# Two heads per stationary operand in the second score pass, its maxima subtracted by a bf16 matmul of three parts, and the experts' counts and lists put in other slots

## The reference: what is computed

```python
h = tok_ref(x, 102, tok_table, pos_table, seg_table)      # gather + position + segment, times 16
h = h + attn_ref(layernorm(h), wq, wk, wv, wgq, wgk, wgv, r_out_w, gate_local_w, gate_remote_w, w_out)
h = h + ffn_ref(layernorm(h), centroids, ln_g, ln_b, w1, b1, w2, b2)
```

## Time and profile before

| | |
|---|---|
| median of three runs | 2784.46 us (2783.8 to 2791.09) |
| the profiled execution | 2778.41 us, span 2776.6 us |
| PE busy | 2597.7 us, 94% of the span, 41512 matmul records |
| DVE busy | 1737.3 us, 63% |
| ACT busy | 1199.2 us, 43% |
| POOL busy | 966.5 us, 35% |
| attention, steady stretch | about 70 to 1690 us, 32 sequences |
| choice for expert 0 alone | about 1695 to 1775 us |
| experts | about 1785 to 2776 us |

### The profile page before, as it was taken

The page is one execution under the profiler, slowest core; times in us unless marked ns, Lnnn a source line. Parts: engine busy times, 40 slices in busy tenths (PEclk is TensorE's granted clock), DMA queues, the critical chain, the costliest instruction groups (busy, mean ns, idle before and its releaser), DMA issues. The chain is left out here.

```text
span 2776.6 us, 97280 instructions
## 1 busy us (share of the span) xinstructions
PE 2597.7 (94%) x41512; PEld 1766.3 (64%) x41512; DVE 1737.3 (63%) x5575; ACT 1199.2 (43%) x2659; POOL 966.5 (35%) x1417
## 2 busy tenths in 40 slices
PE   5999999999999999999999983399999999999998
PEld 3666666666766666666666662266666666666665
DVE  5666666666666666666666656775756667575600
ACT  2444445545444544444444430243333444433342
POOL 4332333433423333334233200134434343444333
PEclk9999999999999999999999995699999999999999
DMA  2110111101101111011010001012121121112020
GB/s 77 24 26 24 28 26 26 26 26 26 26 24 28 26 26 25 25 26 28 24 26 26 24 17 39 16 33 67 34 71 49 50 70 36 66 35 71 27 71 29
DMA packets 62599, 98.67 MB, mean 36 GB/s; under 512 B 13676, under 2 KB 47544, under 8 KB 62168
## 3 DMA queue, kind: packets, MB, share of 16 engines
q0 software_dynamic: 18624, 51.14, 6.9%
q1 hardware_dynamic: 43544, 41.29, 4.5%
HBM read 55.88 MB, written 33.82 MB: 32 GB/s over the span
## 5 line engine op out<-in xcount | busy, mean ns | idle before, releaser
L911 PE MATMUL banks<-hT,w 128*128 128x512 f32 x1024 | 469.8, 606 | 11.2 <-ACT hT L728 10.8
L1180 DVE TENSOR_REDUCE mx<-banks 128x8 f32<-128x1024 f32 x256 | 301.2, 1219 | 128.2 <-PE banks L1022 128.2
L702 ACT ACTIVATE probT<-banks 128x1024 f32<-128x1024 f32 x256 | 259.2, 1026 | 224.8 <-PE banks L1066 224.8
L739 ACT ACTIVATE hid<-banks,b 128x512 f32<-128x512 f32 x256 | 175.8, 687 | 400.9 <-PE banks L911 400.9
L911 PEld LDWEIGHTS banks<-hT,w 128*128 128x128 f32 x1024 | 188.0, 192 | 214.4 <-issue 198.5
L550 POOL TENSOR_TENSOR h<-ve,mhalf 128x2 f32<-128x2 f32 x128 | 92.0, 719 | 648.8 <-DVE ve L1221 648.7
L528 POOL DMA_INDIRECT rows<-in_tok_table,idx_now x132 | 138.4, 1049 | 399.9 <-DVE hres L1158 347.8
L1079 PEld LDWEIGHTS V_ps<-Ve,probT 128*64 128x64 f32 x4096 | 251.6, 139 | 34.6 <-issue 34.6
L1079 PE MATMUL V_ps<-Ve,probT 128*64 128x17 f32 x4096 | 264.4, 212 | 0.1
L1079 PE MATMUL V_ps<-Vo,probT 128*64 128x17 f32 x4096 | 264.4, 212 | 0.0
L593 POOL TENSOR_TENSOR orow<-orow,b 128x256 f32<-128x256 f32 x128 | 134.7, 1052 | 370.7 <-DVE orow L1345 369.6
(11 more groups left out here) (225 smaller groups left out, 5402.7 us busy)
## 6 DMA issues: line engine op xcount, KB each, us to landing
h_rows<-h SPq DMA_DIRECT2D x128, 130.0 KB, 2.0
w<-in_w SPq DMA_DIRECT2D x16, 1024.0 KB, 5.2
Qt<-low SPq DMA_DIRECT2D x512, 2.0 KB
Gq<-lowl SPq DMA_DIRECT2D x256, 2.0 KB
Kt<-units SPq DMA_DIRECT2D x256, 4.0 KB
rows<-in_tok_table,idx_now POOLq DMA_INDIRECT x132, 3.7
out_rows<-orow,idx_cur POOLq DMA_INDIRECT x128, 2.4
Gk<-units SPq DMA_DIRECT2D x64, 1.0 KB
```

The costliest lines, as they stand in the source:

```text
L702: nc.scalar.activation(dst[:, 2 * pair:2 * pair + 2, :], banks[:, 2 * pair:2 * pair + 2, :], ACT.Exp).then_inc(s_exp, 1)
L739: nc.scalar.activation(hid[:, m, :], S_ps[m % 2][:, 0:GT * P], ACT.Gelu_apprx_tanh, bias=b1[:, m:m + 1]).then_inc(s_hid, 1)
L911: mm = nc.tensor.matmul(S_ps[m % 2][:, 0:GT * P], w1[:, c, m * P:(m + 1) * P], hT[g % 2][:, c, :], start=c == 0, stop=c == KC - 1)
L1180: nc.vector.tensor_reduce(tops.rearrange("p (g h) -> p g h", g=2), banks[:, 2 * pair:2 * pair + 2, :].rearrange("p g (h k) -> p g h k", h= ...
```

## The change

Second pass of a query tile (steps 1 to 4). The even and odd head of a pair now share one stationary operand: `Kf`, the keys of all heads with nothing zeroed, is the stationary operand, and `Qt` (now with the other head's rows zeroed, by `c_query`) is streamed for both `j` at once. So 24 product matmuls stand where 48 stood, with twice the columns each. The first pass uses `Qf` (plain scaled queries) as its stationary operand and is otherwise as it was. ACT writes `Qf` and `Kf` besides the two copies of `Qt` and of `Kt` (three copies of 512 columns for each Q or K task instead of two).

The maxima no longer go through a DMA. DVE splits the negative maximum of each query and head into three bf16 parts (high, middle, rest; four instructions right behind the two reductions, in `dve_tops`), MX lays them out on PE (four bf16 matmuls against the identity `identb` instead of one transpose), ACT copies the whole bank to `tops_rows`, and `key_scores` adds them to the scores: for each strip one bf16 matmul of 3 rows, 128 output rows and 512 columns with ones as stationary operand, between the masks and the products. MX waits on the new semaphore `s_tops`. Step 0 keeps the old way under the name ML.

Experts: the radix sums on PE stand one or two slots later, the list has four pieces of 32 tiles (`LC = 4`), and its pieces stand in other slots.

```diff
-            [("MT", 1), ("ET", 0), ("ET", 1), ("WO", 1), ("VAL", 2), ("ET", 2), ("ET", 3), ("MX", 0)],
+            [("MT", 1), ("ET", 0), ("ET", 1), ("WO", 1), ("VAL", 2), ("ET", 2), ("ET", 3), ("ML", 0)],
...
             elif name == "MX":
-                dst = lowl if t == 0 else low[(t - 1) % 2]
-                nc.scalar.activation(dst[:, :], bank[0:LH * TS if t == 0 else H, 0:P], ACT.Copy, scale=-1.0).then_inc(s_mA, 1)
+                nc.scalar.activation(tops_rows[t % 2][:, :, :].rearrange("p n q -> p (n q)"), bank[:, :],
+                                     ACT.Copy).then_inc(s_mA, 1)
...
             elif name == "Q":
+                nc.scalar.activation(Qf[nx][:, t, :], bank[:, :], ACT.Copy, scale=HD ** -0.5)
                 for j in range(2):
-                    ins_ = nc.scalar.activation(Qt[nx][:, j, t, :], bank[:, :], ACT.Copy, scale=HD ** -0.5)
+                    ins_ = nc.scalar.activation(Qt[nx][:, j, t, :], bank[:, :], ACT.Copy, scale=c_query[:, j:j + 1])
...
             elif name == "K":
+                nc.scalar.activation(Kf[nx][:, t, W:], bank[:, :], ACT.Copy)
...
             elif name == "MX":
-                pe.wait_ge(s_max, 2 * (NU * b + t + 1))
-                tops = mxl[:, :] if t == 0 else mx[:, t % 2, :]
-                mm = nc.tensor.transpose(bank[0:LH * TS if t == 0 else H, 0:P], tops, c_ident)
+                pe.wait_ge(s_tops, TS * b + t)
+                for n in range(G):
+                    mm = nc.tensor.matmul(bank[:, n * P:(n + 1) * P], parts3[t % 2][:, n, :], identb[:, :], start=True, stop=True)
...
                 pe.wait_ge(s_max, drained)
-                pe.wait_ge(s_low[u], 16 * 2 * (1 + (TS if u == 0 else KC)) * (b + 1))
+                if u == 0:
+                    pe.wait_ge(s_low, 16 * (2 + 2 * TS) * (b + 1))
+                else:
+                    pe.wait_ge(s_mA, lowered)
...
-                for n in range(G):
-                    j, c = divmod(n, KC)
+                for g in range(G):
+                    nc.tensor.matmul(banks[:, g, :], onesb[32 * g:32 * g + 3, :],
+                                     tops_rows[(t + 1) % 2][32 * g:32 * g + 3, :, :].rearrange("p n q -> p (n q)"),
+                                     start=False, stop=False)
+                for c in range(KC):
                     for g in range(G):
-                        k, q = Kt[par][strip[g], j, c, :], Qt[par][strip[g], j, c, :]
-                        nc.tensor.matmul(banks[side[0], g, n * P:(n + 1) * P], k[:, W + at_:P + at_], q[:, at_:at_ + P],
-                                         start=False, stop=n == G - 1)
-                        nc.tensor.matmul(banks[side[1], g, n * P:n * P + W], k[:, at_:W + at_], q[:, at_:at_ + W],
+                        k, q = Kf[par][strip[g], c, :], Qt[par][strip[g], :, c, :]
+                        out0, out1 = (banks[side[a], g, :].rearrange("p (j c q) -> p j c q", j=2, c=KC)[:, :, c, :]
+                                      for a in range(2))
+                        nc.tensor.matmul(out0, k[:, W + at_:P + at_], q[:, :, at_:at_ + P],
+                                         start=False, stop=c == KC - 1)
+                        nc.tensor.matmul(out1[:, :, 0:W], k[:, at_:W + at_], q[:, :, at_:at_ + W],
                                          start=False, stop=False)
-                    for g in range(G):
-                        k, q = Kt[par][strip[g], j, c, :], Qt[par][strip[g], j, c, :]
-                        mm = nc.tensor.matmul(banks[side[1], g, n * P + W:(n + 1) * P], k[:, P + at_:P + W + at_],
-                                              q[:, at_ + W:at_ + P], start=False, stop=n == G - 1)
+                        mm = nc.tensor.matmul(out1[:, :, W:P], k[:, P + at_:P + W + at_], q[:, :, at_ + W:at_ + P],
+                                              start=False, stop=c == KC - 1)
...
-                 (2, Q0 + 1): [("list", 0)], (2, Q0 + 2): [("list", 1)], (2, Q0 + 3): [("list", 2)],
-                 (3, 0): [("list", 3)], (3, 1): [("list", 4)], (3, 2): [("list", 5)], (3, 3): [("list", 6)],
-                 (3, 5): [("list", 7)]}
+                 (2, Q0 + 2): [("list", 0)], (3, 0): [("list", 1)], (3, 3): [("list", 2)], (3, 6): [("list", 3)]}
...
         for g in range(2):
-            for n, slot in enumerate((2, 5, Q0 + 1, Q0 + 3)):
+            for n, slot in enumerate((3, 7, Q0 + 1, Q0 + 3)):
                 pe_at[g, slot] = [("radix", 4 * g + n)]
...
-            dve_at[g, 6] = [("digit", 4 * g + 1)]
-            dve_at[g, Q0] = [("count", 4 * g + 2)]
+            dve_at[g, Q0] = [("digit", 4 * g + 1), ("count", 4 * g + 2)]
...
+            if s > 0:
+                dve.wait_ge(s_max, 2 * k + 2)
+                top = mx[:, s % 2, :].rearrange("p (g n) -> p n g", g=G)
+                hi, mid, lo = (parts3[s % 2].rearrange("p n (g x) -> p n g x", g=G)[:, :, :, i] for i in range(3))
+                chain(dve, nc.vector.tensor_scalar(hi, top, -1.0, None, ALU.mult), 0)
+                chain(dve, nc.vector.scalar_tensor_tensor(out=left[:, :, :], in0=top, scalar=-1.0, in1=hi,
+                                                          op0=ALU.mult, op1=ALU.subtract), 0)
+                chain(dve, nc.vector.tensor_copy(mid, left[:, :, :]), 0)
+                nc.vector.tensor_tensor(lo, left[:, :, :], mid, ALU.subtract).then_inc(s_tops, 1)
+                dve.wait_ge(s_tops, TS * (k // NU) + s)
```

More of the change, by code:

```diff
@@ L99, in tower @@
     FC = F // P
-    LC = min(8, NT // 8)
+    LC = min(4, NT // 8)
     LT = NT // LC
@@ L221, in tower @@
         Kt = [sba(f"Kt{j}", [P, 2, KC, W + S]) for j in range(2)]
+        Qf = [sba(f"Qf{j}", [P, KC, S]) for j in range(2)]
+        Kf = [sba(f"Kf{j}", [P, KC, W + S]) for j in range(2)]
         Gq = [sba(f"Gq{j}", [P, 2, S]) for j in range(2)]
@@ L232, in tower @@
         latT = sba("latT", [P, G, 512])
-        low = [sba(f"low{j}", [H, P]) for j in range(2)]
+        parts3 = [sba(f"parts3{j}", [P, G, P], BF16) for j in range(2)]
+        left = sba("left", [P, G, G])
+        identb = sba("identb", [P, P], BF16)
+        tops_rows = [sba(f"tops_rows{j}", [P, G, P], BF16) for j in range(2)]
         lowl = sba("lowl", [LH * TS, P])
@@ L304, in tower @@
         s_max = sem("s_max")
-        s_low = [sem(f"s_low{u}") for u in range(NU)]
+        s_tops = sem("s_tops")
+        s_low = sem("s_low")
         s_ST = sem("s_ST")
@@ L461, in store @@
                         scored = n // 2
[L462 to L466, removed]
+                        if scored == 0:
+                            sp.wait_ge(s_S, 2 * (NU * b + 1))
                             for j in range(2):
[L468 to L472, removed]
+                                sp.dma_start(Gk[q % 2][HD * (1 - j)::32, j, :], units[:, :]).then_inc(s_low, 16)
                     for task in half:
                         name, s = task
-                        if name == "MX" and m.here(task):
+                        if name == "ML" and m.here(task):
                             sp.wait_ge(s_mA, m.out(task))
                             for j in range(2):
-                                if s == 0:
-                                    for t in range(TS):
-                                        sp.dma_start(Gq[q % 2][HD * (1 - j)::32, j, t * P:(t + 1) * P],
-                                                     lowl[j * TS + t::2 * TS, :]).then_inc(s_low[s], 16)
-                                else:
-                                    for c in range(KC):
-                                        sp.dma_start(Qt[q % 2][HD * (1 - j)::32, j, c, (s - 1) * P:s * P],
-                                                     low[(s - 1) % 2][2 * j + c::2 * KC, :]).then_inc(s_low[s], 16)
+                                for t in range(TS):
+                                    sp.dma_start(Gq[q % 2][HD * (1 - j)::32, j, t * P:(t + 1) * P],
+                                                 lowl[j * TS + t::2 * TS, :]).then_inc(s_low, 16)
                     for task in half:
@@ L1112, in sequence @@
                         if s == 0:
-                            key_scores(b - 1, 1 - par, NU - 1, drained)
+                            key_scores(b - 1, 1 - par, NU - 1, drained, m.out_before(("MX", NU - 1)))
                         else:
-                            key_scores(b, par, s - 1, drained)
+                            key_scores(b, par, s - 1, drained, m.out(("MX", s - 1)) if s > 1 else None)
                     half(2 * s + 1)
```

35 lines of the change are left out of this document (22 added, 13 removed).

## The result

The changed kernel takes **2972.03 us** (2964.87 to 2974.62), the one before 2784.13 us in the same comparison: a ratio of 1.0668, 95% interval 1.064 to 1.0696. It is slower, as forecast, but by 188 us and not by 64, and outside the range of 2806 to 2900.

A forecast was written before the change was run, and what follows sets the result against it. PE was taken to bound the kernel. Split +54, second pass with MX +20, ACT +2 and experts -12 made +64 us, which gave 2848 us on the scale of the measured medians, range 2806 to 2900 us.

The forecast's parts named there:

- What bounds the kernel: In attention PE is busy 54.03 of 54.40 us, so each microsecond PE is made to wait is lost.
- the sum itself: Whole kernel: terms 54 + 20 + 2 - 12 = +64 us, read at a granted clock of 1.00.
- The split on DVE: Between reductions and MX: four instructions, 0.80 us, stall PE at steps 3 and 4; +54 us, bounds 38 to 78.
- the rival with POOL: At step 4 POOL, normalizing a tile, slows DVE's split: the 78 us bound, 2872 us; no separate chance given.
- MX on PE: Four bf16 matmuls and a shape change take 0.33 us instead of 0.20: +0.13 us each.
- The three parts: Second pass on PE, between masks and products: four new matmuls cost 0.42 us with shape changes, 0.24 if those are free.
- The products: Second pass on PE: 24 matmuls with the same 4096 columns take 1.03 us instead of 1.42, -0.39 us each.
- The first rival: PE is bound by the number of matmuls: products take 0.71 us, 2769 us in all; chance 0.05.
- the second, strips held up in program order: A second matmul on a tile delays the strips behind: products take 2.16 us, 2993 us in all; chance 0.08.
- ACT: Third copy per Q and K task and MX's longer copy stay hidden from PE, except +2 us at the start.
- Experts: Later radix sums cut PE's 16.0 us of waits for DVE's counts to 4: -12 us, bounds -16 and 0.

The follow-up runs named there:

- filler run: Changed kernel with 16 useless matmuls of 128 columns on PE ahead of the wait at MX of steps 3 and 4: 2881.67 us.
- MX behind RT: Changed kernel with MX of steps 1 to 4 moved behind the second pass of its step, right behind RT or first in its half: 2818.43 us.
- experts alone: Kernel before with only the experts' part of the change, four list pieces and the new slots: 2767.57 us.
- the run with halves: MX behind RT, plus each strip's three-part matmul cut into two of 64 output columns: 2789.99 us.
- products by rounds: Changed kernel with the third product of all strips issued behind the first two of all strips: 2935.15 us.
- the parts between the products: The run with halves, with products issued by rounds and the eight half matmuls moved between the products of c = 0 and c = 1: 2777.85 us.
- the old matmuls: Kernel before with DVE's four split instructions added and MX of steps 1 to 4 waiting for them, parts unread: 2879.27 us.

## Why the prediction was wrong, step by step

The runs split the 188 us, each part by the difference of two medians. They come from four series, in which the kernel before had medians of 2784.1 to 2787.0 us, so each part is good to some 3 us:

| part | from | us | predicted |
|---|---|---|---|
| clock falling | change less filler run | +90.4 | no term |
| PE's wait for the split | filler run less MX behind RT | +63.2 | +54 |
| second pass, MX, ACT | MX behind RT less experts alone | +50.9 | +22 |
| experts | experts alone less before | -16.6 | -12 |

The rows are differences of whole runs. The first holds the 5 us by which MX comes earlier in the filler run; the second also holds MX's shorter 0.23 us behind RT instead of 0.31, some 10 us.

**What bounds the kernel: right.** "A microsecond that PE is made to wait is one lost" was right as far as it went; behind some of the waits such a microsecond cost more than one.

**The failed step is the sum itself, which priced PE's work at the clock of the earlier trace rows.** The prediction read "granted clock of 1.00" there and kept it for a kernel that would idle PE twice a sequence. No term and no rival has the 1.2 GHz level in it. The falls behind the stalls took 85 to 90 us. Without them, as in the filler run, the change takes 2881.67 us, inside the range.

The kernel before had shown the fall, among the experts, in the very waits that were read as a sum: seven of the 19 are of 1.9 us, and behind two of these seven, at 2072 and at 2567 us, the granted clock is 0.50. The first of the two, PE's wait and the window behind it (kernel before):

```profile
2070.85 0.18 PE L840 MATMUL M_ps<-counts,onesb 128*128 128x15 bf16 x1 [1.92 <-DVE hits L1255]
2072.06:2075.47 3.41, 3.41 (x5) 1.33 (x4) 3.34 (x25) 0.69 (x1) 0.80 (x1) 0.50 0.30 81
```

The page TensorE: Matmul & The Clock Gate of the Trainium skill says in Part 1, under HAM oscillation, that a wait in every tile of a loop can make the clock fall each time anew. The trace agrees that the fall comes again and again, in 31 stretches; but not every stall is followed by one.

**The split on DVE: right, a little too cheap.** Wait and place were as predicted: steps 3 and 4, 63 waits. From start to start the four instructions are 0.24, 0.22, 0.41 or 0.24 and 0.26 apart, where I took 0.20 from the earlier trace rows: 1.07 and 1.11 us idle, not 0.80. The CAST is the longest, 241 ns in the mean; it takes 0.20 at step 3 and 0.37 at step 4, where POOL normalizes a tile beside it. That is the rival with POOL, at 0.17 us and not at the 0.25 of its bound; whether POOL is the cause was not tested. 71.2 us of waits lie within my bounds of 38 to 78.

**MX on PE: right.** 0.31 us in the change (forecast 0.33); 0.23 where it stands behind RT and no change of shape follows.

**The three parts: right.** 0.33 and 0.11 more on the masks, 0.44 against 0.42; the run with halves shows that the shape is what costs.

**The products: wrong, 1.33 us instead of 1.03.** That is 0.30 x 128 = 38 us, the second thing that the sum had wrong. That "below some thirty matmuls columns decide" failed: 24 matmuls with the columns of a first pass take 0.36 us more than its 16. 0.05 of it is the order (products by rounds) and 0.04 went with the halves. With the parts between the products the pass of 1.77 less masks (0.47) and parts (0.22) leaves 1.08, nearly the forecast; that columns decide wherever instructions come in time is my reading of it, not shown. The first rival, bound by number (0.71), and the second, strips held up in program order (2.16), fell too. Against the second the prediction had read one row too early: by count, the record at 1003.84 is the last of the second round. The next one of L1060, at 1003.87, is the first of the third, and still ahead of the L1066 at 1003.91.

**ACT: hidden, as said.** MX's copy of 512 columns takes 597 ns (mean of 128); of PE's waits in the change one, of 0.4 us, names K's copies and none Q's, until MX was moved to the end of a half.

**Experts: right in the time, half right in the cause.** -16.6 us against -12, just past the bound of -16 (-19.4 within the series of that run). From the first L911 to PE's last matmul, kernel before and change:

```profile
1785.28:2766.90 981.62, 955.52 (x4307) 631.16 (x4307) 567.69 (x2452) 395.27 (x753) 386.72 (x374) 0.99 0.16 50
1994.13:2960.60 966.47, 948.34 (x4307) 631.27 (x4307) 570.06 (x2424) 396.05 (x753) 412.94 (x374) 1.00 0.16 51
```

Of these 15 us 8 are PE's idle time: the waits for counts fell from 16.0 to 5.1 us, as forecast, and 3.0 us of waits for the ties are new. The other 7 are PE's busy time, which the prediction did not have. Up to 3.4 of them are the two stretches at half clock named above, which are gone; where the rest went was not followed. That the total came so near the forecast is in part luck.

## What to carry to other kernels

When PE is the bound and never idle, a wait can cost twice: once as idle time, and again if the granted clock falls behind it. Price a new stall with a range that has the 1.2 GHz level in it, and look at the clock column of short windows behind the waits that are there already: in a long one, two short falls hardly show. If a chain on DVE must stand between two PE stages, give PE other work there: moving MX behind the next pass took back 154 of 188 us, and even throw-away matmuls took back 90.

## What was not expected of the hardware

- Stalls of 1.1 us, two in a sequence of 54 to 58 us, were followed by stretches at the 1.2 GHz level in most sequences of the change (31 stretches, 32 sequences), in about half with the old matmuls (17), and by none between 80 and 1750 us when PE was kept busy with matmuls whose result nobody reads. Seven waits of 1.9 us in the kernel before were followed by two.
- Changing the shape of the array between 32x64 and 3x128 matmuls cost 0.11 us each way, the same as half of the 512 columns that those matmuls stream.
- Moving long bf16 matmuls from ahead of the small fp32 products to between them shortened the pass by 0.21 us in the one kernel (some 0.05 of it the order) and by 0.06 us in the other. The fastest kernel of the study, 2758.72 us, is the one before with the experts' part and this. The new second pass at its best, 2777.85 us, loses to the experts' part alone, 2767.57 us.
